# Cross-attention with layer norm: the last batch's output projection begun before its last value products, and its layer norm done query tile by query tile

## The reference

```python
Q = (q @ Wq + bq).reshape(b, s, H, DH).transpose(0, 2, 1, 3)
K = (k @ Wk + bk).reshape(b, s, H, DH).transpose(0, 2, 1, 3)
V = (v @ Wv + bv).reshape(b, s, H, DH).transpose(0, 2, 1, 3)
scores = jnp.einsum('bhqd,bhkd->bhqk', Q, K) / jnp.sqrt(jnp.float32(DH))
scores = scores * mask
attn = jax.nn.softmax(scores, axis=-1)
ctx = jnp.einsum('bhqk,bhkd->bhqd', attn, V)
ctx = ctx.transpose(0, 2, 1, 3).reshape(b, s, H * DH)
out = ctx @ Wo + bo
x = q + out
mu = jnp.mean(x, axis=-1, keepdims=True)
var = jnp.var(x, axis=-1, keepdims=True)
return (x - mu) * jax.lax.rsqrt(var + LN_EPS) * gamma + beta
```

## Time and profile before

| | us |
|---|---|
| median of 3 runs | 2202.15 |
| lowest and highest run | 2201.57, 2203.34 |
| the profiled execution, its own time | 2204.18 |
| its span, from the first to the last instruction | 2202.4 |
| TensorE busy, share of the span | 2099.0, 95% |
| VectorE busy, share | 1947.7, 88% |
| ScalarE busy, share | 1787.5, 81% |
| GpSimd busy, share | 1030.6, 47% |

### The profile page before, as it was taken

One profiled execution on the slowest core, in us unless ns is written; L12 is line 12 of the kernel. 1 busy time (PEld: TensorE's weight loads), 2 busy tenths in 40 slices (PEclk: granted clock), 3 DMA queues, 4 the chain that ended last, 5 costly groups with the idle time before them and its releaser, 6 DMA issues.

```text
span 2202.4 us, 37555 instructions
## 1 busy us (share of the span) xinstructions
PE 2099.0 (95%) x12348; PEld 883.9 (40%) x12348; DVE 1947.7 (88%) x4283; ACT 1787.5 (81%) x3809; POOL 1030.6 (47%) x1576
## 2 busy tenths in 40 slices
PE   2689999999999999999999999999999999999985
PEld 1234444444444444444444444444444444444432
DVE  6779899999989999998999999899999989999882
ACT  3669798797978879797887969889797988979791
POOL 2116264362735437273553737355372635537244
PEclk9799999999999999999999999999999999999997
DMA  6368879797897978799797979979797897979683
GB/s 224 72 120 167 179 139 212 134 192 155 176 201 128 215 136 187 158 168 206 131 208 142 184 160 175 201 136 198 147 186 158 168 211 132 196 144 184 136 162 87
DMA packets 1117603, 364.00 MB, mean 165 GB/s; under 512 B 1073504, under 2 KB 1073504, under 8 KB 1117408
## 3 DMA queue, kind: packets, MB, share of 16 engines
q1 hardware_dynamic: 1114288, 361.58, 82.0%
q10 hardware_dynamic: 3120, 0.01, 0.1%
HBM read 76.30 MB, written 16.78 MB: 42 GB/s over the span
## 4 chain that ended last, share of the span: by engine, by line
PE 91%; DVE 4%; DMA 2%; POOL 1%; ACT 1%; issue 1%; POOLq 0%; ACTq 0%; DVEq 0%; SPq 0%
PE fill_ps L390 21%; PE fill_ps L391 19%; PE fill_ps L392 19%; PE score_ps L443 16%; PE ctx_ps L464 15%; DVE score_ps L917 1%; DMA pT<-p 1%; DVE p L931 1%; DMA bv_col<-in_L_xattn_bv 1%; DVE small L799 1%; PE ctx_ps L377 0%; ACT probs L615 0%; DVE wk L836 0%; DVE wq L836 0%; POOL acc L1261 0%
## 5 line engine op out<-in xcount | busy, mean ns | idle before, releaser
L615 ACT ACTIVATE probs<-score_ps,neg_max 128x512 f32<-128x512 f32 x1024 | 692.2, 687 | 154.4 <-POOL neg_max L1216 146.0
L917 DVE CUSTOM_DVE_ANT_0 score_ps<-score_ps,mask_sb,small 128x512 f32<-128x512 f32 x1024 | 724.0, 754 | 100.1 <-PE score_ps L443 97.1
L629 ACT ACTIVATE p<-probs,inv_sum 128x512 f16<-128x512 f32 x1024 | 674.3, 720 | 100.6 <-DVE inv_sum L925 89.6
L931 DVE SCALAR_TENSOR_TENSOR p<-probs,inv_sum,p 128x512 f16<-128x512 f32 x896 | 697.9, 816 | 12.0 <-ACT p L629 10.2
L1216 POOL TENSOR_SCALAR neg_max<-row_max 128x2 f32<-128x2 f32 x512 | 155.3, 303 | 689.8 <-DVE row_max L917 689.7
L443 PE MATMUL score_ps<-k,q 64*128 64x512 f16 x3072 | 388.4, 379 | 11.3 <-ACT probs L615 5.7
L464 PE MATMUL ctx_ps<-pT,v 128*64 128x512 f16 x3072 | 359.8, 384 | 18.5 <-DMA pT<-p 14.5
L464 PEld LDWEIGHTS ctx_ps<-pT,v 128*64 128x64 f16 x3072 | 165.6, 110 | 205.2 <-issue 76.5
L1222 POOL TENSOR_SCALAR down_sum<-row_sum 128x4 f32<-128x4 f32 x256 | 76.2, 298 | 357.2 <-ACT probs L615 349.2
L443 PEld LDWEIGHTS score_ps<-k,q 64*128 64x128 f16 x3072 | 127.5, 94 | 251.5 <-issue 99.3
L615 ACT ACTIVATION_READ_ACCUMULATOR probs<-score_ps,neg_max 128x1 f32 x1024 | 210.4, 205 | 0.0
(11 more groups left out here) (91 smaller groups left out, 2960.4 us busy)
## 6 DMA issues: line engine op xcount, KB each, us to landing
raw<-in_xt SPq DMA_DIRECT2D x64, 256.0 KB, 3.4
raw<-in_ct SPq DMA_DIRECT2D x64, 256.0 KB, 3.5
mask_sb<-in_mask_Bx1xSxS_fk SPq DMA_DIRECT2D x64, 256.0 KB, 3.6
acc<-in_x SPq DMA_DIRECT2D x64, 256.0 KB, 3.7
out<-acc SPq DMA_DIRECT2D x64, 256.0 KB, 2.8
pT<-p SPq DMA_TRANSPOSE x512, 4.6
wq_staged<-in_L_xattn_Wq SPq DMA_DIRECT2D x4, 512.0 KB, 7.3
wk_staged<-in_L_xattn_Wk SPq DMA_DIRECT2D x4, 512.0 KB, 11.2
```

The lines of the kernel that those rows point to most:

```text
L615: nc.scalar.activation(probs[:, i % E_TILES, :], score_ps[:, i % 4, :], ACT.Exp, bias=neg_max[:, p % 2, i:i + 1], accum_out=row_sum[:, p % ...
L629: nc.scalar.activation(p16[:, q, a, 0, :], probs[:, i % E_TILES, :], ACT.Copy, scale=inv_sum[:, p % 2, i:i + 1]).then_inc(p_rounded, 1)
L917: nc.vector.tensor_tensor_reduce(out=score_ps[:, i % 4, :], in0=score_ps[:, i % 4, :], in1=mask_sb[:, q, :], scale=score_scale, scalar=-3. ...
L931: nc.vector.scalar_tensor_tensor(out=p16[:, q, a, 1, :], in0=probs[:, i % E_TILES, :], scalar=inv_sum[:, p % 2, i:i + 1], in1=p16[:, q, a, ...
```

## The change

In the last batch alone, TensorE makes six of the eight pairs' products for query tiles 0 and 1 behind the last scores and ahead of `values(6)`, the same for tile 2 between `values(6)` and `values(7)`, and the products of pairs 6 and 7 for the three tiles behind `values(7)`. O2 of this batch goes to bank 0, so that three partial sums can stand at once. Each part waits for `ctx_split` of each of its pairs. O3 is filled whole, in the closing stage.

The closing stage gets programs of its own. VectorE takes statistics and `bn_aggr` tile by tile and multiplies by gamma and adds beta itself; GpSimd does `add_bo` for tiles 1 to 3 and then the four small instructions once for each tile, on one column; ScalarE standardizes each tile as its numbers come. SyncE's order stays. The other batches are untouched.

```diff
+        def fill_bank(n, kind, k):
+            return 0 if (n, kind, k) == (LAST, "O", 2) else FILL_BANK[f"{kind}{k}"]
...
-        def batches(eng, body):
-            body(None, None, 0, False)
+        def batches(opening, body, closing):
+            opening()
             body(None, 0, 1, True)
             for b in range(1, B - 1):
                 body(b - 1, b, b + 1, False)
             body(B - 2, B - 1, None, False)
-            body(B - 1, None, None, False)
+            closing()
...
+            def closing():
+                load_acc(LAST, range(1, QT))
+                store(LAST, range(QT))
...
+            def output_part(n, k, pairs):
+                bank_no = fill_bank(n, "O", k)
+                cut = slice(k * P, (k + 1) * P)
+                if pairs.start == 0 and bank_no in users:
+                    pe.wait_ge(*users[bank_no])
+                for j in pairs:
+                    pe.wait_ge(ctx_split, pair_no(n, j))
+                    mm = products(fill_ps[:, bank_no, :], [ctx16[:, j, l, cut] for l in (0, 1)],
+                                  [w16["o"][:, j, l, :] for l in (0, 1)], j == 0, j == PAIRS - 1)
+                if pairs.stop == PAIRS:
+                    mm.then_inc(out_ready, 1)
+                    users[bank_no] = fill_read(n, "O", k)
...
                 if here is not None:
                     values(here, 5)
                     scores(here, 7, range(2, 4))
+                if nxt is None and here is not None:
+                    for k in range(2):
+                        output_part(here, k, range(0, 6))
...
+                if nxt is None and here is not None:
+                    output_part(here, 2, range(0, 6))
                 if here is not None:
                     values(here, 7)
...
-                if here is not None:
+                if here is not None and nxt is not None:
                     fill(here, "O", 0)
+                if here is not None and nxt is None:
+                    for k in range(3):
+                        output_part(here, k, range(6, PAIRS))
...
+            def closing():
+                fill(LAST, "O", 3)
...
+            def closing():
+                for q in range(QT):
+                    act.wait_ge(shift_done, LAST + q + 1)
+                    nc.scalar.activation(acc[:, q, :], acc[:, q, :], ACT.Identity, scale=rstd[:, q:q + 1],
+                                         bias=shift[:, q:q + 1]).then_inc(centered, 1)
...
+            def closing():
+                def statistics(q):
+                    take_stats(LAST, range(q, q + 1))
+                    dve.wait_ge(stats_done, out_no(LAST, q))
+                    nc.vector.bn_aggr(moments[:, q, :], stats[:, q, :]).then_inc(moments_done, 1)
+
+                def finish(q):
+                    i = out_no(LAST, q)
+                    dve.wait_ge(centered, i)
+                    nc.vector.tensor_tensor(acc[:, q, :], acc[:, q, :], gamma_b[:, :], ALU.mult).then_inc(scaled, 1)
+                    dve.wait_ge(scaled, i)
+                    nc.vector.tensor_tensor(acc[:, q, :], acc[:, q, :], beta_b[:, :], ALU.add).then_inc(normed, 1)
+
+                statistics(0)
+                evacuate(LAST, "O", 1)
+                statistics(1)
+                evacuate(LAST, "O", 2)
+                statistics(2)
+                finish(0)
+                finish(1)
+                evacuate(LAST, "O", 3)
+                statistics(3)
+                finish(2)
+                finish(3)
...
+            def closing():
+                add_bo(LAST, range(1, QT))
+                for q in range(QT):
+                    one, done = slice(q, q + 1), LAST + q + 1
+                    pool.wait_ge(moments_done, out_no(LAST, q))
+                    nc.gpsimd.tensor_tensor(var_eps[:, one], moments[:, one, 1], eps4[:, one], ALU.add).then_inc(eps_added, 1)
+                    nc.gpsimd.tensor_tensor(neg_mean[:, one], moments[:, one, 0], minus4[:, one],
+                                            ALU.mult).then_inc(mean_negated, 1)
+                    pool.wait_ge(eps_added, done)
+                    nc.gpsimd.tensor_tensor(rstd[:, one], var_eps[:, one], half4[:, one], ALU.pow).then_inc(rstd_done, 1)
+                    pool.wait_ge(mean_negated, done)
+                    pool.wait_ge(rstd_done, done)
+                    nc.gpsimd.tensor_tensor(shift[:, one], neg_mean[:, one], rstd[:, one], ALU.mult).then_inc(shift_done, 1)
```

More of the change, by code:

```diff
@@ L351, in body, with opening @@
                     transpose_probs(nxt, 0, range(1, 2))
-            batches(sp, body)
+            def opening():
+                body(None, None, 0, False)
+            def closing():
+                load_acc(LAST, range(1, QT))
+                store(LAST, range(QT))
+            batches(opening, body, closing)
             for q in range(QT):
@@ L396, in fill @@
             def fill(n, kind, k):
-                bank_no = FILL_BANK[f"{kind}{k}"]
+                bank_no = fill_bank(n, kind, k)
                 bank = fill_ps[:, bank_no, :]
@@ L560, in body, with opening @@
                     bias_output()
-            batches(pe, body)
+            def opening():
+                body(None, None, 0, False)
+            def closing():
+                fill(LAST, "O", 3)
+            batches(opening, body, closing)
         @block.scalar
@@ L586, in evacuate @@
             def evacuate(n, kind, k):
-                bank = fill_ps[:, FILL_BANK[f"{kind}{k}"], :]
+                bank = fill_ps[:, fill_bank(n, kind, k), :]
                 if kind == "V":
@@ L788, in body, with opening @@
                     round_weight("o")
-            batches(act, body)
+            def opening():
+                body(None, None, 0, False)
+            def closing():
[3 more added lines that the diff above has]
+                                         bias=shift[:, q:q + 1]).then_inc(centered, 1)
+            batches(opening, body, closing)
         @block.vector
@@ L1176, in body, with opening @@
                     add_bias_output()
-            batches(dve, body)
+            def opening():
+                body(None, None, 0, False)
+            def closing():
[20 more added lines that the diff above has]
+                finish(3)
+            batches(opening, body, closing)
         @block.gpsimd
@@ L1397, in body, with opening @@
                     negate_max(nxt, 2, range(1, 2))
-            batches(pool, body)
+            def opening():
+                body(None, None, 0, False)
+            def closing():
[11 more added lines that the diff above has]
+                    nc.gpsimd.tensor_tensor(shift[:, one], neg_mean[:, one], rstd[:, one], ALU.mult).then_inc(shift_done, 1)
+            batches(opening, body, closing)
 _INS = ['x', 'ctx_1024', 'mask_Bx1xSxS2_fk1', 'L0_xattn_Wq', 'L0_xattn_bq', 'L0_xattn_Wk', 'L0_xattn_bk',
```

## The result

The changed kernel takes 2183.26 us, the median of four runs (2183.07 to 2185.55), against 2201.89 us (2201.57 to 2203.34): 18.6 us less, a ratio of 0.9916 with a 95% interval of 0.9900 to 0.9932. The interval is wide: 15.0 to 22.0 us, so that the medians alone can't tell 18.6 from the 20.6 forecast. The forecast was 2181.6 us, between 2179.2 and 2185.0. The profiled execution took 2185.55 us, its span is 2183.8 us.

The account below looks back on a forecast made before the run. TensorE, busy 95% of the span, bounds the kernel; only the tail could move. Its steps ended the span at 2181.8 instead of 2202.4, 20.6 us off: profiled 2204.18 becomes 2183.6, median 2181.6, range 2179.2 to 2185.0 us.

Parts of the forecast that it names:

- likeliest case: Tail as summed, stand paid for by half clock, VectorE in series behind O3: 2180.7 to 2182.6 us, chance 0.50.
- sum: Tail followed engine by engine: span ends at 2181.8 instead of 2202.4, 20.6 us off, median 2181.6.
- third one: Closing stage, VectorE and GpSimd slow each other throughout, half clock at its longest: 2182.6 to 2185.0 us, chance 0.24.
- Ahead of pair 6: TensorE behind the last scores: 15 products, a 3.5 us stand, then 21 products in 4.5 us, to 2152.0.
- forecast's signs: Expected in the trace after: 3.5 us stand, pair 6 near 2153.5, pair 7 near 2160.5, O3 near 2173, last pass near 2179.3.
- The clock: TensorE behind the 3.5 us stand: half clock costs 1.95 us (1.35 to 2.55), pair 7's value products start at 2160.5.
- stand of 3.16 us: A TensorE wait elsewhere in the kernel before, followed by half clock: 12 score products in 2.74 instead of 1.54 us.
- transposes of pair 7: Ahead of pair 7's value products: they take 4.34 us from 2154.70, so TensorE could start at 2159.29 as before.
- Behind pair 7: Closing stage: pair 7 read from 2165.5, VectorE 1.62 us a tile, O3 out at 2173.3.
- GpSimd: Closing stage: `add_bo` ends at 2167.31, then small instructions take 1.3 us on one column, 2.0 for tile 3.
- The passes: VectorE's gamma and beta passes: 0.75 us each, 1.5 a tile; last ends at 2179.3, span at 2181.8.
- three rivals: Tail: VectorE and GpSimd slow each other (0.24), half clock never ends, no change (0.03), dear VectorE passes, beyond 2185 (0.01).

Follow-up runs that it names:

- e1: TensorE's part of the change alone, the other engines' closing stage as in the kernel before; 2190.74 us, 13.0 less than the kernel before beside it.
- e7: Changed kernel with ScalarE taken out of the closing stage: two fused VectorE passes, GpSimd makes rstd alone; 2180.90 us.
- e5: Changed kernel with the eight gamma and beta passes back on GpSimd, behind each tile's small instructions; 2189.60 us.
- e6: The changed kernel measured once more, unaltered; 2184.27 us, 18.0 less than the kernel before beside it.
- e4: Changed kernel with nine of tile 0's 18 early products moved into earlier gaps of TensorE; 2183.87 us.
- e3: Changed kernel with 15 unused products filling TensorE's stand for the low plane of pair 5; 2182.43 us.
- e2: The new closing stage alone, TensorE's order and banks as in the kernel before; 2194.02 us, 9.8 less than the kernel before beside it.
- e8: Changed kernel with all four tiles' six pairs early, fused VectorE passes for tiles 1 to 3, tile 0's gamma and beta on GpSimd; 2179.38 us.

## Why the prediction was right, step by step

By its steps the likeliest case came, and its sum can be laid beside the trace when 1.8 us (2141.00 - 2139.22) are taken off each time of the changed kernel. By its time it did not: 2183.26 lies above the 2180.7 to 2182.6 of that case, in the range of the third one, in which VectorE and GpSimd slow each other throughout, and that isn't what the trace shows. So the steps were right by their reasons, while the time lies within the whole range only because the range had room for a case that did not come.

- *Ahead of pair 6*: 15 products and a stand of 3.33 us, released by VectorE's L983; forecast 3.5. The value products of pair 6 started at 2153.5, where the forecast's signs had them (the sum has 2152.0 and the clock's price, up to 1.95, on top).
- *The clock*: it fell in the stand and took 1.5 us from the products behind it (21 products in 6.05 us against 4.5), forecast 1.95. Pair 7 started at 2160.2, forecast 2160.5. What the sum counted in full is a toss: the same stand of 3.33 us left the clock alone in e1 and e7 and lost it in the change, e5 and e6. The stand of 3.16 us that the forecast leaned on is no surer: in the opening, which is the same in all twelve kernels, it was followed by half clock in eleven profiles, but in e4's the first seven products behind it took 1.04 us at a granted clock of 1.00. The half clock's price in the end time is 0.6 us (e3), forecast 0.9. The transposes of pair 7 didn't quite stay: where TensorE waits for them, it starts 20.07 us behind the last scores' start in the kernel before, 20.1 in e7, 20.4 in e1 and e3. In the change they had landed before TensorE came.
- *Behind pair 7*: evacuation of tile 0 at 2165.25 (2165.5), O3 read at 2173.4 (2173.3). VectorE's 1.62 us a tile was right for tiles 1 and 2, tile 0 took 1.95, with 0.26 of idle time ahead of the second evacuation. Pair 7 was 0.3 early and tile 0 took 0.3 longer: that O3 fits to 0.1 us is two small misses cancelling.
- *GpSimd*: `add_bo` didn't hold tile 0, because its moments came at 2166.9 and `add_bo` had ended at 2166.3, not 2167.3. The forecast took the loads ahead of it as not moved; but `add_bo` ended 27.9 to 28.2 us behind the last scores' start in the kernel before (both profiles) and e2, and 26.8 to 27.2 in the others. Why the loads come sooner there isn't shown; in the sum it cost nothing. One column's set took 1.19 us (1.3) beside an evacuation and 1.97 (2.0) under passes.
- *The passes*: 0.66 to 0.70 us, 2.72 from the first start to the last end for the four of tiles 0 and 1, 1.36 a tile (1.5). The last ended at 2179.4 (2179.3), the span at 2182.0 (2181.8).

The gain was 18.6 us in the runs (18.0 when measured again), not 20.6, and the time 1.7 above the forecast. Two things that stand in no step of the sum can make this up. Everything ahead of the last scores was taken as equal, and in the changed kernel's profile 1.7 us more went to half clock at pair 4. And the sum started from a single execution of the kernel before, with 5.33 us for the last value products, where another had 4.13. The pair of profiles that has neither gives 18.9 us by the tail alone, so the second would do without the first; which of the two the unprofiled runs paid isn't shown, and the interval of the medians holds 20.6 as well. The three rivals in which the passes are slow or the clock never returns had no part in it: the slowest pass took 0.70 us.

The Trainium skill's rule on the clock ("TensorE: Matmul & The Clock Gate", "HAM oscillation — how this bites in real kernels"), that TensorE left idle while it waits for data comes back at half clock and runs the next products cold, agrees with every long stand in the tails of these traces (5.28 us in e4, 6.49 us and more in the kernel before and e2, half clock each time) and with three of five stands of 3.33 us. Its rule that GpSimd contends with VectorE instructions that have two SBUF inputs ("GPSIMD Engine Reference", "Key points") agrees with the power: 0.99 us under passes, against 0.57 beside an evacuation, which has one input in PSUM, and 0.55 with VectorE idle (tiles 2 and 3 of e5).

What stays open: whether the unprofiled runs of the change lose anything by half clock at pair 4, since they carry no clock by stretch; and whether the thin stretch at pair 4 is dearer in the changed kernel more often than in others.

## What to carry to other kernels

In a tail where one engine waits twice for data and another ends in a long series, split the last accumulation so that what is ready is done inside the waits, and then look which engine has become the series: here it was VectorE, so that the next 3.9 us moved on TensorE brought 1.2 (0.4 behind pair 7, the rest by the clock), and a wait taken out of VectorE's chain 1.5. Forecast such an edit by the stretch that it touches, not by the whole time; two profiles of one unchanged kernel differed by 1.2 us in that stretch alone. Put small cross-engine instructions where the other engine isn't in a pass of two SBUF inputs.

## What the runs showed of the hardware

The same TensorE program behind the same stand of 3.33 us ran at full clock in two executions and at half in three, so a stand of this length has no fixed price. The stretch ahead of pair 4's value products has no stand over 0.8 us, and the clock was lost there too, in three of eleven executions. A power on GpSimd took 1.02 us for four columns and 0.55 to 0.57 for one, and 0.99 to 1.07 for one under VectorE's passes (the change, e7, e8). A VectorE pass over float32 with two SBUF inputs took 0.66 to 0.70 us, the fused one with a column operand 0.72 to 0.75 (0.93 once, beside a wide pass on GpSimd), against 1.26 for a pass on GpSimd.
